# Packing attention scores into four 32-row groups, splitting queries in place, and unrolling the loop

## The reference, cut to what matters

```python
qh = split_heads(norm(x) @ Wq + bq)        # 4 x 16 heads x 512 tokens x 8
kh = split_heads(ctx @ Wk + bk)            # 4 x 16 heads x 77 keys x 8
vh = split_heads(ctx @ Wv + bv)
attn = softmax(qh @ kh^T / sqrt(8))        # per head, over the 77 keys
x = x + tanh(g) * (concat(attn @ vh) @ Wo + bo)
```

## Time and profile before

| what | value |
|---|---|
| median of three timed runs | 836.13 us |
| lowest and highest | 834.06 and 837.66 us |
| span of the profiled execution | 838.4 us |
| TensorE busy | 681.6 us, 81% of the span |
| VectorE busy | 629.8 us, 75% |
| ScalarE busy | 409.6 us, 49% |
| GpSimd busy | 414.6 us, 49% |
| mean granted TensorE clock | 0.874 of full speed |

### The profile page before, as it was taken

One profiled execution on the slowest core, in us unless ns is written; L12 is line 12 of the kernel. 1 busy time (PEld: TensorE's weight loads), 2 busy tenths in 40 slices (PEclk: granted clock), 3 DMA queues, 4 the chain that ended last, 5 costly groups with the idle time before them and its releaser, 6 DMA issues.

```text
span 838.4 us, 13196 instructions
## 1 busy us (share of the span) xinstructions
PE 681.6 (81%) x3114; PEld 544.3 (65%) x3114; DVE 629.8 (75%) x2092; ACT 409.6 (49%) x751; POOL 414.6 (49%) x450
## 2 busy tenths in 40 slices
PE   4423210089999999999999879999998999999996
PEld 2211110077788888888888559998866888888884
DVE  6779999778777777777777786767585777777774
ACT  2534300034565656565656554445454565656563
POOL 5657730026566666666666451110134666666663
PEclk9755555557999999999999979999599999999999
DMA  5365421124877777777777100000417676657661
GB/s 131 72 138 143 124 68 32 34 52 94 162 153 144 158 140 156 141 149 148 153 144 156 34 10 1 1 0 0 94 33 158 138 159 142 156 140 158 143 145 51
DMA packets 79209, 89.14 MB, mean 106 GB/s; under 512 B 44181, under 2 KB 56838, under 8 KB 75716
## 3 DMA queue, kind: packets, MB, share of 16 engines
q1 hardware_dynamic: 72118, 78.37, 44.8%
q0 software_dynamic: 4320, 9.68, 4.1%
q10 hardware_dynamic: 2734, 0.69, 0.4%
HBM read 79.84 MB, written 8.70 MB: 106 GB/s over the span
## 4 chain that ended last, share of the span: by engine, by line
PE 70%; DVE 19%; issue 5%; DMA 2%; ACT 2%; POOL 1%; DVEq 0%; POOLq 0%; ACTq 0%
PE bank L1000 14%; PE bank L1002 13%; PE bank L1001 13%; PE bank L1136 7%; PE bank L1134 6%; PE bank L1133 6%; PE bank L1064 4%; DVE arena L1432 3%; PE bank L1046 2%; DVE arena L1428 2%; DVE arena L1389 2%; DVE arena L1381 1%; DVE arena L1429 1%; PE bank L939 1%; DVE arena L1390 1%
## 5 line engine op out<-in xcount | busy, mean ns | idle before, releaser
L694 POOL TENSOR_TENSOR act_lo<-arena,act_hi 128x512 fp32r<-128x512 f32 x232 | 300.2, 1294 | 201.9 <-ACT act_hi L831 201.9
L1644 DVE TENSOR_TENSOR bank<-arena,bank 128x512 f32<-128x512 f32 x232 | 160.7, 693 | 105.2 <-PE bank L1002 72.3
L843 ACT ACTIVATE arena<-bank 128x512 f32<-128x512 f32 x232 | 138.9, 599 | 178.1 <-PE bank L1002 176.0
L1000 PE MATMUL bank<-xn_hi,w_hi 128*128 128x512 f32 x464 | 187.3, 404 | 3.6 <-DVE arena L1652 3.6
L1002 PE MATMUL bank<-xn_lo,w_hi 128*128 128x512 f32 x464 | 184.8, 398 | 0.0
L1001 PE MATMUL bank<-xn_hi,w_lo 128*128 128x512 f32 x464 | 184.2, 397 | 0.0
L1652 DVE TENSOR_TENSOR arena<-bank,arena 128x512 f32<-128x512 f32 x232 | 160.4, 691 | 21.5 <-DVE bank L1644 9.2
L831 ACT ACTIVATE act_hi<-arena 128x512 fp32r<-128x512 f32 x232 | 145.2, 626 | 15.7 <-DVE arena L1652 15.7
L1000 PEld LDWEIGHTS bank<-xn_hi,w_hi 128*128 128x128 f32 x464 | 88.4, 191 | 27.4 <-DVE arena L1652 5.4
L1002 PEld LDWEIGHTS bank<-xn_lo,w_hi 128*128 128x128 f32 x464 | 88.3, 190 | 22.0
L1001 PEld LDWEIGHTS bank<-xn_hi,w_lo 128*128 128x128 f32 x464 | 88.7, 191 | 20.8
(11 more groups left out here) (194 smaller groups left out, 963.8 us busy)
## 6 DMA issues: line engine op xcount, KB each, us to landing
arena<-scr_mask SPq DMA_DIRECT2D x94, 512.0 KB, 6.4
scr_w<-prep_out POOLq DMA_DIRECT2D x25, 192.0 KB, 2.2
w_raw<-scr_w SPq DMA_DIRECT2D x25, 192.0 KB, 6.5
arena<-scr_one SPq DMA_DIRECT2D x6, 512.0 KB, 6.0
w_raw<-in_L_ffn_expert_gate_k SPq DMA_DIRECT2D x32, 64.0 KB, 6.1
w_raw<-in_L_ffn_expert_up_k SPq DMA_DIRECT2D x32, 64.0 KB, 5.9
w_raw<-in_L_ffn_expert_down_k SPq DMA_DIRECT2D x64, 32.0 KB, 5.4
prep_in<-in_L_ffn_wg POOLq DMA_DIRECT2D x21, 64.0 KB, 2.3
```

The source lines that it names most:

```text
L694: nc.gpsimd.tensor_tensor(act_lo[:, k % 2, :], act_a[:, k % 2, :], act_hi[:, k % 2, :].bitcast(F32), ALU.subtract).then_inc(FF[f]["alo"], 1)
L843: nc.scalar.activation(act_s[:, k % 2, :], ps[4 + k % 2][:], ACT.Silu).then_inc(FF[f]["silu"], 1)
L1000: nc.tensor.matmul(out, w_h, x_h, start=start, stop=False)
L1644: nc.vector.tensor_tensor(ps[6 + i][:], act_s[:, i, :], ps[6 + i][:], ALU.mult).then_inc(FF[f]["t"], 1)
```

## The change

The heads are grouped by the 32 feature rows in which they lie: four groups of four heads. `kbd` now has four copies of the keys, not sixteen: in copy h, each group of 32 rows keeps the eight rows of its h-th head (`rowmask`, made by one VectorE reduction of `headmask`). A matmul of rows 32r to 32r+31 of a query tile with the same rows of `kbd` gives the 308 columns of group r, in bank r. So a tile's scores are twelve matmuls of 32 rows and 308 columns (three passes, four groups each) where there were nine of 128 rows (six of 462 columns and three of 308). They are issued together, pass by pass, ahead of the rest of the step, and wait for both subtractions of the tile before.

Banks 0 to 3 are now two tensors of two banks, and VectorE takes two maxima and two subtractions, each over two banks (616 columns). Transposed exponentials have banks 4 and 7; the third group reuses bank 4 and moves to the next step, behind that step's scores. The halves of the queries are written over `xn_hi` and `xn_lo` in place, TensorE reads them there, and GpSimd's copies are gone; its bias is added per batch in four instructions. All four engines' loops are written out for 16 tiles. VectorE's normalisation and the addition to x now follow both subtractions.

```diff
-    EXP_BANKS = [3, 4, 7]
+    EXP_BANKS = [4, 7, 4]
...
-                nc.gpsimd.tensor_copy(qs_hi[:, j, :], qT_hi[:, tok].bitcast(F32))
-                nc.gpsimd.tensor_copy(qs_lo[:, j, :], qT_lo[:, tok].bitcast(F32)).then_inc(s_qs, 1)
...
+                for b in range(B):
+                    xb = x_res[:, TPB * b:TPB * (b + 1), :]
+                    nc.gpsimd.tensor_tensor(xb, xb, bo_all[:].unsqueeze(1).broadcast_to([P, TPB, P]), ALU.add).then_inc(s_bias, 1)
...
-                if 2 <= g < 2 + HEADS:
+                if 2 <= g < 2 + RHEADS:
...
-                                                   ACT.Copy, scale=headmask[:, h:h + 1])
+                                                   ACT.Copy, scale=rowmask[:, h:h + 1])
...
+                def scores(i):
+                    b, tok = i // TPB, slice(P * i, P * (i + 1))
+                    pe.wait_ge(s_qlo, b + 1)
+                    if i >= 1:
+                        pe.wait_ge(s_sub, 2 * i)
+                    for n, (q_all, k_all) in enumerate(((xn_hi, kbd_hi), (xn_lo, kbd_hi), (xn_hi, kbd_lo))):
+                        for r in range(RG):
+                            rows = slice(RROWS * r, RROWS * (r + 1))
+                            mm = nc.tensor.matmul(ps[r][:, 0:RCOLS], q_all[rows, tok],
+                                                  k_all[rows, b].rearrange("p h k -> p (h k)"), start=n == 0, stop=n == 2)
+                            if n == 2 and r % 2 == 1:
+                                mm.then_inc(s_sc, 1)
...
+                for i in range(TILES + 2):
+                    if i == 2:
+                        pe.wait_ge(s_qlo, CHUNKS)
+                    if i < TILES:
+                        scores(i)
+                    if i >= 2:
+                        exp_back(i - 2, 2)
+                    if i >= 3:
+                        av_back(i - 3)
+                    if i >= 2:
+                        values(i - 2)
+                    if i >= 3:
+                        project(i - 3)
+                    if 1 <= i <= TILES:
+                        exp_back(i - 1, 0)
+                        exp_back(i - 1, 1)
...
+                    for p in range(2):
+                        dve.wait_ge(s_sc, 2 * i + p + 1)
+                        nc.vector.tensor_reduce(smax[:, j, heads_of(p)].rearrange("p (a h) -> p a h", a=2), score_pair(p),
+                                                AX_X, ALU.max).then_inc(s_mx, 1)
+                    if i >= 2:
+                        dve.wait_ge(s_tr, RT * (i - 1))
+                    for p in range(2):
+                        dve.wait_ge(s_mx, 2 * i + p + 1)
...
+                        nc.vector.tensor_tensor(to, score_pair(p), most.broadcast_to([P, 2, RHEADS, KEYS]),
                                                 ALU.subtract).then_inc(s_sub, 1)
...
+                for i in range(TILES):
+                    if i >= 2:
+                        copy_exp(i - 2, 2)
+                    if i >= 3:
+                        copy_av(i - 3)
+                    if i >= 1:
+                        copy_exp(i - 1, 0)
+                        copy_exp(i - 1, 1)
+                    exp(i)
```

More of the change, by code:

```diff
@@ L865, in copy_av, with copy_exp @@
                     nc.scalar.activation(avT, ps[6][:, 0:P], ACT.Copy).then_inc(s_avc, 1)
[L867 to L868 removed]
+                def copy_exp(i, r):
+                    j = i % 2
+                    if r == 0 and i >= 2:
                         act.wait_ge(s_av, i - 1)
[L870 to L874, removed]
@@ L1022, in attention @@
             def attention():
-                pe.wait_ge(s_kbd, HEADS)
+                pe.wait_ge(s_kbd, RHEADS)
                 pe.wait_ge(s_vf, 16 * sum(LAST_HEAD[c] + 1 - FIRST_HEAD[c] for c in range(FT)))
                 pe.wait_ge(s_epad, 1)
-                def scores(i, b, j, r):
-                    h0, h1 = HSPLIT[r]
-                    if r == 0:
[L1030 to L1038, removed]
@@ L1042, in exp_back, with values @@
+                def values(i):
+                    b, j = i // TPB, i % 2
+                    total = ps[5][:, 0:HEADS * (HD + 1)]
+                    if i >= 1:
+                        pe.wait_ge(s_nrm, i)
+                    nc.tensor.matmul(total, zeros[0:1, 0:P], zeros[0:1, 0:HEADS * (HD + 1)], start=True, stop=False)
                     for r in range(RT):
-                        if not (isinstance(i, int) and i == 0):
-                            pe.wait_ge(s_ev, RT * i + r - RT + 1)
+                        pe.wait_ge(s_ev, RT * i + r + 1)
@@ L1045, in exp_back @@
                         for c in range(HT * r, min(HT * (r + 1), FT)):
[L1046 to L1067, removed]
@@ L1077, in project @@
                     nc.tensor.matmul(ps[6][:, P:2 * P], avT, w4[:, 3, :], start=True, stop=True).then_inc(s_wo, 1)
[L1079 to L1088, removed]
-                        if r == 1 and not (first and i < 3):
-                            project(i - 3)
-                    if not (first and (i < 1 or i > TILES)):
-                        exp_back(i - 1, 1 - j)
-                for i in range(TPB):
+                for i in range(TILES + 2):
                     if i == 2:
                         pe.wait_ge(s_qlo, CHUNKS)
-                    step(i, 0, 0, i % 2)
-                with pe.Fori(1, B) as t:
-                    for q in range(TPB):
-                        step(TPB * t + q, t, t - 1 if q < 2 else t, q % 2)
-                step(TILES, None, B - 1, 0)
-                step(TILES + 1, None, B - 1, 1)
+                    if i < TILES:
[11 more added lines that the diff above has]
+                        exp_back(i - 1, 1)
                 turn(3, 0)
-                av_back(TILES - 1, 1)
+                av_back(TILES - 1)
                 project(TILES - 1)
```

159 lines of the change are left out of this document (68 added, 91 removed).

## The result

The changed kernel takes 863.9 us (median of four executions, 857.0 to 869.61) where the kernel before took 835.91 (834.06 to 837.66) beside it: a ratio of 1.0335, with a 95% interval of 1.0285 to 1.0386. The forecast was 899 and slower. The direction is right, the size is not: 28 us were lost where 63 were forecast. The profiled execution's span is 867.9 us, 29.5 longer than before, and its mean granted clock is 0.823 against 0.874.

A forecast was written before the change was run, and what follows sets the result against it. TensorE bounds the attention; at the low clock, start +5.5, twelve steps +51.4, tile 15's step +4.3 and two scoreless steps +2.3 total +63: 838.4 to 901.7 us profiled, 899 timed; range 826 to 912.

The forecast's parts named there:

- What bounds the kernel: Attention's steady part: TensorE is the bound, busy for all of 24.00 us at clock 1.00; VectorE for 16.81.
- Scores at 2.4 GHz: A tile's score block at the high clock: 1.3 us, ends 0.5 and 2.3; step 5.1 us, down from 5.77.
- The rest of the step: TensorE's work in an attention step other than scores, at the high clock: 3.82 us.
- Scores at 1.2 GHz: A tile's score block at the low clock: 2.4 us, ends 1.0 and 4.0; step 10.05 us, 4.28 more.
- Which clock: Whole attention stage: the low clock throughout likeliest, chance 0.52, giving 899 us, 879 to 921 by the score block's ends.
- toggling: Rival, attention: the clock toggles or comes late; 852 and 872 us, 845 to 885 with the ends; chance 0.14.
- The clock comes up early and stays: Rival, attention: high clock by the third tile and held; 828 us, ends 818 and 841; chance 0.26.
- In turn: Rival: score groups run one after another; 838 to 841 us at high clock (chance 0.03), 921 at low (0.05).
- VectorE the bound: Rival, attention: VectorE's step of about 4.3 us limits the gain to 818 us; no separate chance given.
- The start: First attention tiles: tile 2's scores wait for the second subtraction, +0.8 us; tile 3's scores +5.5 at low clock.
- The covers: Third exponential group's later bank, removed GpSimd copies and unrolled loop: 0; up to 0.5 us a tile if one fails.
- the steps behind tile 15: End of attention at low clock: tile 15's own step +4.3 us, the two steps without scores +2.3.

The follow-up runs named there:

- experiment 1: The changed kernel with its twelve score matmuls a tile over all 128 rows instead of 32 (scores not the reference's): 854.0 us, ratio 1.022.
- experiment 5: The changed kernel plus 24 unread wide matmuls behind tile 0's scores and six of 512 columns in the next gap: 857.5 us, ratio 1.0256.
- experiment 7: The changed kernel plus the long starting burst (24 and six wide matmuls) and eight unread 128-row, 360-column matmuls in each tile's `values`: 843.55 us, ratio 1.0116.
- experiment 11: The changed kernel with 128-row scores (not the reference's), the score block cut in two, half behind the first eight of `values`: 841.81 us, ratio 1.0095.
- experiment 9: The changed kernel plus the long starting burst and eight unread 360-column matmuls a tile, on 32 rows instead of 128: 921.25 us.
- experiment 12: The changed kernel with its packed 32-row score block cut in two, half behind the first eight of `values`: 899.28 us, ratio 1.0774.
- experiment 3: The changed kernel plus four unread 128-row, 360-column matmuls in each tile's `values`, no starting burst: 903.55 us.
- experiment 4: The changed kernel plus twelve unread 512-column matmuls behind tile 0's scores and four of 360 columns in each tile's `values`: 899.4 us, ratio 1.0758.
- experiment 6: The changed kernel plus the long starting burst (24 and six wide matmuls) and four unread 128-row, 360-column matmuls in each tile's `values`: 899.73 us.
- experiment 8: The changed kernel plus the long starting burst and four unread 360-column matmuls a tile, on 32 rows instead of 128: 906.23 us, ratio 1.085.
- experiment 2: The changed kernel plus twelve unread matmuls of 128 rows and 512 columns behind tile 0's scores: 862.96 us, ratio 1.0329.

## Why the prediction was right in direction and wrong in size

**What bounds the kernel: right.** TensorE is busy for all of the steady part, before and after, and neither VectorE nor a transfer sets the pace.

**Scores at 2.4 GHz: the mechanism right, the size low in my range.** 0.63 us, where I took 1.3 with 0.5 as an end. The weight loads that I priced at 0.10 each overlap across groups; a pass of four comes in 0.14, near the 0.167 of one. Ahead of the second pass 0.11 is added and behind the third 0.10, inside the 0.15 that I allowed for a change of row shape; the first is hardly the shape's, since experiment 1's full-row block has 0.07 there too (its first pass of four takes 0.64 us, its second 0.57). The estimate from the Trainium skill ("TensorE: Matmul & The Clock Gate", Part 3) was 0.65 us, and the trace agrees, with 0.63. The rest of the step, which I had left at 3.82, is the term that was wrong here: it is 4.25. The two errors nearly cancel, 4.88 us for my 5.1, and that is luck.

**Scores at 1.2 GHz: this term was mis-sized.** 1.07 us for my 2.4, near the bottom of my ends. I had taken 0.2 us for each of twelve loads; a pass of four took 0.26. The rest of a low step is 9.02 - 1.07 = 7.95 us, 0.3 more than my 7.65. A low step is 9.02 and not 10.05, and 12 x 9.02 - 69.1 = 39.1 us where I had 51.4: 12.3 us of the error.

**Which clock: the step that failed.** I wrote that no stretch of the attention looks like the two where it rose, and that the likeliest was the low clock throughout. It was up in part of six of the twelve steps; it rose behind eight transposes, the score block and two transposes in a row, and fell in the scoreless stretch. That gave back 108.2 - 90.5 = 17.7 us, the larger error. I had named this run of work as what would most likely prove me wrong, and gave toggling 0.14; its 845 to 885 holds the 863.9. Why it rose in some steps and not in others with the same work stays open. The other half of the argument stands: with the packed scores the small work does not carry the clock, and with eight full-row matmuls more it does (experiments 5 and 7).

**"The clock comes up early and stays": fell.** Experiment 5 raised it early, and it fell 4.7 us after TensorE's last pause. The rule of the Trainium skill ("TensorE: Matmul & The Clock Gate", the table of "Why this matters for your kernels") that idle gaps between bursts be avoided is not enough here: TensorE is busy for 60.00 of 60 us at a clock of 0.56, and the clock falls in them.

**In turn, and VectorE the bound: both fell**, by the 0.26 and 0.14 us of a pass and by VectorE's 15.7 us of waiting.

**The start: the wait right, the delay too small.** Tile 1's scores come at 500.29, released by the second subtraction as forecast, against 498.13 before: 2.2 us late for my 0.8. Some 0.7 us are that wait. The other 1.4 were already there when VectorE began tile 0's maxima, at 497.24 against 495.88: TensorE did the last query projection and tile 0's scores at 0.50 here and at 1.00 before, which I had not looked at. Tile 3 is 4.7 us late (I had 5.5), since tile 2's step took 8.27 us for my 9.3, and the steps behind tile 15 cost 5.9 (6.6).

**The covers: held.** The third group's bank, GpSimd's copies and the unrolled loop show nowhere: TensorE has no idle time from 512 to 572 us.

The terms add up to within 0.2 us. The profiled execution was forecast at 901.7 and took 867.9, 33.8 less: 12.3 by the low step, 17.7 by the rises, 0.8 at the start, 0.7 at the end, and the 2.5 us elsewhere that was not followed up. By the true price of the low step alone, with the clock low throughout, the forecast would have been 899 - 12.3, about 887, and still slower than before: the direction needed the clock below 1.00 for much of the stage, not low throughout.

## What to carry to other kernels

Before taking wide matmuls out of a TensorE-bound stage, read which of them the granted clock rests on: here packing would have saved 0.9 us in each step, some 11 in all, at the clock of before, and the kernel lost 28 instead. A step priced at one clock is worth nothing until the trace, or one run, shows that the clock stays with the new mixture, and a busy share of 100% does not show that. In this stage spreading the full-row matmuls over the step helped (12 us in experiments 1 and 11), and narrow-row ones did not stand in for them (7 and 9, 11 and 12). And a step is compared with the same step of before: the first ones and the last lack some of the work.

## What the runs showed that I had not expected

**Full rows kept the clock, 32 rows did not.** Eight fillers of 360 columns a step held the clock at 1.00 with 128 rows and left it at 0.56 with 32, 843.6 us against 921.3. With four fillers it was 0.50 with 128 rows and 0.56 with 32, in one profiled execution each, so more rows did not mean more clock there.

**More work can be worse, and I can't say why.** In the profiled executions of the four kernels whose low step took 10.21 to 10.22 us (3, 4, 6 and 12) the clock never rose in the steps from tile 3 on. The changed kernel, with low steps of 9.02 us, rose in every third step at first, and so did experiments 8 and 9, with low steps of 11.07 and 12.27 us. So a longer low step doesn't by itself keep the clock down, and neither does a filler. What is special about 10.2 us, or about the work in those four, stays open; so does why four fillers made the kernel slower than none, by 36 to 42 us in the medians and by 19 and 28 between the fastest executions of 3 and 6 (876.02, 880.71) and those without filler (857.0, 852.31).

**Executions of one kernel spread.** The kernel before stays within 2 to 6 us; the changed one covers 12.6 us (857.0 to 869.61), and experiments 3 and 6 cover 30 and 22. Experiment 2, whose clock also rises and falls, stays within 0.7, so not every such kernel spreads. Where one may, one execution is not a measurement.
